# Half-position scans: lane sums completed by a product on TensorE and copied to their place by ScalarE

## What is computed

```python
# layer 0: four directions k over the positions (rows, columns, and both reversed)
dA = exp(dt[..., None] * A)
h = h * dA + (dt * u)[..., None] * B          # per position
y = einsum('bkdn,bkn->bkd', h, C)             # sum over the 16 states n
# the four y are brought back to row order and added; D * u is added for every direction
# layer 1: one direction over the positions
y = y + xin * D                               # then y * silu(z), out projection
```

## Time and profile before

| | us |
|---|---|
| median of 3 runs | 5808.86 (5805.29 to 5818.28) |
| profiled execution | 5813.53 |
| its span, first to last instruction | 5811.2 |
| TensorE busy (matmuls) | 4773.5 (82%) |
| VectorE busy | 4627.5 (80%) |
| GpSimd busy | 4111.9 (71%) |
| ScalarE busy | 3426.8 (59%) |
| granted TensorE clock, mean | 0.919 |

### The profile page before, as it was taken

One profiled execution on the slowest core, in us unless ns is written; L12 is line 12 of the kernel. 1 busy time (PEld: TensorE's weight loads), 2 busy tenths in 40 slices (PEclk: granted clock), 3 DMA queues, 4 the chain that ended last, 5 costly groups with the idle time before them and its releaser, 6 DMA issues. The chain is left out here.

```text
span 5811.2 us, 66280 instructions
## 1 busy us (share of the span) xinstructions
PE 4773.5 (82%) x20263; PEld 3262.6 (56%) x20263; DVE 4627.5 (80%) x4745; ACT 3426.8 (59%) x5199; POOL 4111.9 (71%) x3131
## 2 busy tenths in 40 slices
PE   5767686788889887778898887778988888777998
PEld 2222233236677745656676755665767764664787
DVE  5999947968999947986999965995999984996544
ACT  3434354337777756655777856764878765763222
POOL 3999926948999926975999953993999962993121
PEclk8898898888999998888999998888999999888999
DMA  5555505427778715645787833653878751662110
GB/s 213 213 210 190 182 28 185 155 93 268 264 267 280 248 46 191 216 152 187 265 270 263 281 116 128 222 188 124 282 265 275 259 195 55 212 219 86 41 49 28
DMA packets 340470, 1076.86 MB, mean 185 GB/s; under 512 B 31522, under 2 KB 123266, under 8 KB 332808
## 3 DMA queue, kind: packets, MB, share of 16 engines
q1 hardware_dynamic: 340104, 1072.52, 53.0%
HBM read 1058.72 MB, written 13.68 MB: 185 GB/s over the span
## 5 line engine op out<-in xcount | busy, mean ns | idle before, releaser
L958 PE MATMUL banks<-ident,prod 128*128 128x128 f32 x4752 | 780.9, 291 | 503.6 <-DVE prod L1172 388.5
L958 PEld LDWEIGHTS banks<-ident,prod 128*128 128x128 f32 x4752 | 566.0, 147 | 802.5 <-DVE prod L1172 616.6
L476 PE MATMUL banks<-prod,ident 128*128 128x512 f32 x972 | 563.7, 720 | 304.4 <-DVE prod L618 242.0
L1163 DVE TENSOR_TENSOR_SCAN banks<-banks,h 128x512 f32<-128x512 f32 x594 | 724.0, 1219 | 79.5 <-POOL h L1113 53.3
L1113 POOL TENSOR_TENSOR h<-lane,Bb 128x512 f32<-128x512 f32 x576 | 723.0, 1272 | 81.8 <-DMA Bb<-half_rows 57.3
L1054 ACT ACTIVATE banks<-lane,A 128x512 f32<-128x512 f32 x864 | 581.3, 686 | 283.5 <-DVE prod L1172 113.9
L534 ACT ACTIVATE banks<-delta_first,A 128x1024 f32<-128x1024 f32 x288 | 321.9, 1118 | 582.6 <-DVE prod L618 482.2
L1172 DVE TENSOR_TENSOR prod<-banks,half_C_a 128x512 f32<-128x512 f32 x792 | 548.0, 692 | 108.8 <-DVE banks L1163 2.9
L476 PEld LDWEIGHTS banks<-prod,ident 128*128 128x128 f32 x972 | 195.6, 219 | 665.4 <-DVE prod L618 414.0
L992 PE MATMUL banks<-Cb,w_a 128*128 128x256 f32 x2304 | 553.8, 380 | 0.0
L1123 POOL TENSOR_TENSOR h<-h,half_C_a 128x512 f32<-128x512 f32 x360 | 461.4, 1282 | 81.6 <-DVE h L1163 64.9
(11 more groups left out here) (382 smaller groups left out, 10936.2 us busy)
## 6 DMA issues: line engine op xcount, KB each, us to landing
Bb<-half_rows SPq DMA_DIRECT2D x576, 512.0 KB, 4.4
Cb<-half_rows SPq DMA_DIRECT2D x288, 512.0 KB, 4.5
w_a<-w_in SPq DMA_DIRECT2D x256, 576.0 KB, 6.3
half_C_a<-half_rows SPq DMA_DIRECT2D x160, 512.0 KB, 6.6
Bb<-rows SPq DMA_DIRECT2D x144, 512.0 KB, 4.2
Cb<-rows SPq DMA_DIRECT2D x144, 512.0 KB, 3.8
w_b<-w_in SPq DMA_DIRECT2D x128, 576.0 KB, 6.5
C_first<-rows SPq DMA_DIRECT2D x40, 1024.0 KB, 8.1
```

The lines of the kernel that those rows point to most:

```text
L476: mm = eng.matmul(ps[:, c, :], m.ident[:, :], src[:, cols(c)], start=n == 0, stop=added(s) == (i + 1) * N, skip_group_check=True)
L958: mm = eng.matmul(ps[:, 0, at], src[:, at], m.ident[:, :], start=n == 0 and k == 0, stop=added(s) == (i + 1) * N, is_transpose=True, skip_ ...
L1163: eng.tensor_tensor_scan(flip(to), flip(slot(s)), flip(m.dBu[:, s % DRIVES, :]), initial, ALU.mult, ALU.add).then_inc(st.scanned, 1)
```

## The change

`back` gets a fifth product: the transposed-back sum stays open in its PSUM group, and a full product with the identity, or with the identity scaled by D, adds the base (`u`, `xin` or the sum so far) to it. ScalarE makes the scaled identity (`scale`, a new resident tensor `scaled`, behind `copy_sum` in step 3) for the lanes that have a D term, 6 of 24 in layer 0 and all of layer 1. `take` moves from VectorE to ScalarE, behind the decay of step 8 (TAKE_AT was 7), and is a plain copy from the bank to its place. For the turned directions the order of positions in the bank stays as it is, and both the base on TensorE and the destination on ScalarE are read and written through a view with a stride of 32 elements. The waits for the previous user of the same place (`taken`, TILES lanes back) move to TensorE.

```diff
-    COPY_AT, BACK_AT, TAKE_AT, SUM_AT, DELTA_AT = 3, 4, 7, 8, 4
+    COPY_AT, BACK_AT, TAKE_AT, SUM_AT, DELTA_AT = 3, 4, 8, 8, 4
...
@@ back, on TensorE
                 for k in range(HALF // P):
                     at = slice(k * P, (k + 1) * P)
-                    mm = eng.matmul(bank("sum", i)[:, at], m.turned_sum[:, at], m.ident[:, :], start=k == 0,
-                                    stop=k == HALF // P - 1, is_transpose=True, skip_group_check=True)
-                mm.then_inc(st.back, 1)
+                    eng.matmul(bank("sum", i)[:, at], m.turned_sum[:, at], m.ident[:, :], start=k == 0, stop=False,
+                               is_transpose=True, skip_group_check=True)
+                x, j, c = lane(i)
+                if x.scale is not None:
+                    eng.wait_ge(st.scaled, scaled(i) + 1)
+                if i >= TILES:
+                    eng.wait_ge(st.taken, i - TILES + 1)
+                eng.matmul(x.view(bank("sum", i)), (m.ident if x.scale is None else m.scaled)[:, :], x.base(j, c), start=False,
+                           stop=True, skip_group_check=True).then_inc(st.back, 1)
...
@@ ScalarE
+            def scale(i):
+                x, j, _ = lane(i)
+                if x.scale is not None:
+                    if scaled(i):
+                        eng.wait_ge(st.back, i)
+                    eng.activation(m.scaled[:, :], m.ident[:, :], ACT.Identity, scale=x.scale(j)).then_inc(st.scaled, 1)
+
+            def take(i):
+                x, j, c = lane(i)
+                eng.wait_ge(st.back, i + 1)
+                eng.activation(x.to(j, c), x.view(bank("sum", i)), ACT.Copy).then_inc(st.taken, 1)
...
                     decay(s)
                     if i and n == COPY_AT:
                         copy_sum(i - 1)
+                        scale(i - 1)
+                    if i and n == TAKE_AT:
+                        take(i - 1)
...
                 if s == STEPS - 1:
                     copy_sum(LANES - 1)
+                    scale(LANES - 1)
+                    take(LANES - 1)
...
@@ VectorE
-            def take(i):
-                x, j, c = lane(i)
-                eng.wait_ge(st.back, i + 1)
-                if i >= TILES:
-                    eng.wait_ge(st.taken, i - TILES + 1)
-                x.take(eng, j, c, bank("sum", i)).then_inc(st.taken, 1)
...
-                    if n == TAKE_AT and i:
-                        take(i - 1)
...
-                if s == STEPS - 1:
-                    take(LANES - 1)
...
@@ layer 0's views (input_tile and sum_tile are u and ys at [:, j, cols(c)])
+            def turned_tile(j, c):
+                w = HALF // HH
+                return ys[:, j, :].rearrange("p (h w) -> p w h", w=WW)[:, c * w:(c + 1) * w, :]
...
+            def turned(y):
+                return y.rearrange("p (w h) -> p w h", h=HH)
...
-                    order = [(0, take_first), (2, take_more), (1, take_turned), (3, take_turned)]
+                    order = [(0, Named(base=input_tile, to=sum_tile, scale=skip_0, view=plain)),
+                             (2, Named(base=sum_tile, to=sum_tile, scale=None, view=plain)),
+                             (1, Named(base=turned_tile, to=turned_tile, scale=None, view=turned)),
+                             (3, Named(base=turned_tile, to=turned_tile, scale=None, view=turned))]
```

More of the change, by code:

```diff
@@ L732, in lane, with scaled @@
         return directions[d], i % TILES, c
+    def scaled(i):
+        return sum(lane(b)[0].scale is not None for b in range(i))
     held = [m.held[:, b, :] for b in range(HELD)]
@@ L2223, in build @@
                 ("kin", [P, CT, 3 * RANK], F32), ("kout", [P, C], F32), ("A0", [P, K0 * N * CT], F32),
-                ("A1", [P, N * DT1], F32), ("w0x", [P, K0, CT, BC + R0], F32), ("lowk", [P, K0 * C + DI], F32),
+                ("A1", [P, N * DT1], F32), ("w0x", [P, K0, CT, BC + R0], F32), ("lowk", [P, K0 * C + DI], F32), ("scaled", [P, P], F32),
                 ("proj1", [P, FT, RANK], F32), ("w1x", [P, DT1, BC + R1], F32)])
@@ L2237, in build @@
                        "back", "taken", "loaded", "hidden", "gelu", "down", "evicted", "accumulated", "ahead",
-                       "w1_0", "w1_1", "w2_0", "w2_1", "aside", "gates", "row", "late_row", *(f"b{i}" for i in range(4)), *(f"c{i}" for i in range(N // 2)))
+                       "w1_0", "w1_1", "w2_0", "w2_1", "aside", "gates", "row", "late_row", "scaled", *(f"b{i}" for i in range(4)), *(f"c{i}" for i in range(N // 2)))
         s_scan.b = [s_scan[f"b{i}"] for i in range(4)]
@@ L2316, in first_image, with plain @@
                     lane_scans(p, scan_tensors(scans, "first"), s_scan, directions, lanes, rows, turn=(u, ut))
+            def plain(y):
+                return y
             def half_scan_tensors(stack, name):
@@ L2404, in shared_scans, with tile, skip @@
                     w_out = tensors(nc, scans, [(f"w_out_{name}", [P, DT1, C], F32)])[f"w_out_{name}"]
-                    def take_tile(eng, t, c, y):
+                    def tile(t, c):
+                        return xin[:, t, cols(c)]
+                    def skip(t):
                         d = VEC["D1"][0] + t
-                        return eng.scalar_tensor_tensor(out=xin[:, t, cols(c)], in0=xin[:, t, cols(c)],
-                                                        scalar=m.vec[:, d:d + 1], in1=y, op0=ALU.mult, op1=ALU.add)
+                        return m.vec[:, d:d + 1]
                     def decay_1(t, n):
@@ L2415, in shared_scans @@
                     mamba = [Named(kts=[xin[:, t, :] for t in range(DT1)], wx=lambda t: m.w1x[:, t, :], rank=R1,
-                                   turned=False, reverse=False, A=decay_1, dt_at=K0 * C, take=take_tile)]
+                                   turned=False, reverse=False, A=decay_1, dt_at=K0 * C, base=tile, to=tile, scale=skip,
+                                   view=plain)]
                     guests = [(slice(0, QUARTER), slice(L - QUARTER, L))]
@@ L2425, in shared_scans, with input_tile, sum_tile, skip_0 @@
                         p.last = Named(all=s_out.all + s_moved.all)
[L2427 to L2434, removed]
-                w = HALF // HH
-                v = ys[:, j, :].rearrange("p (h w) -> p h w", w=WW)[:, :, c * w:(c + 1) * w]
-                return eng.tensor_tensor(v, v, y.rearrange("p (w h) -> p h w", h=HH), ALU.add)
+            def input_tile(j, c):
+                return u[:, j, cols(c)]
+            def sum_tile(j, c):
+                return ys[:, j, cols(c)]
+            def turned_tile(j, c):
+                w = HALF // HH
+                return ys[:, j, :].rearrange("p (h w) -> p w h", w=WW)[:, c * w:(c + 1) * w, :]
+            def skip_0(j):
+                return m.Dsum[:, j:j + 1]
+            def turned(y):
+                return y.rearrange("p (w h) -> p w h", h=HH)
             def decay_0(k):
@@ L2448, in scans @@
                     g = Named(g, un=un, x=m.x, **expert_tensors(fused, name + "0"))
-                    order = [(0, take_first), (2, take_more), (1, take_turned), (3, take_turned)]
+                    order = [(0, Named(base=input_tile, to=sum_tile, scale=skip_0, view=plain)),
+                             (2, Named(base=sum_tile, to=sum_tile, scale=None, view=plain)),
+                             (1, Named(base=turned_tile, to=turned_tile, scale=None, view=turned)),
+                             (3, Named(base=turned_tile, to=turned_tile, scale=None, view=turned))]
                     directions = [Named(kts=[(ut if k % 2 else u)[:, t, :] for t in range(CT)],
                                         wx=lambda t, k=k: m.w0x[:, k, t, :], rank=R0, turned=k % 2 == 1,
-                                        reverse=k >= 2, A=decay_0(k), dt_at=k * C, take=take) for k, take in order]
+                                        reverse=k >= 2, A=decay_0(k), dt_at=k * C, **take) for k, take in order]
                     guests = [(slice(q, q + QUARTER), slice(q, q + QUARTER)) for q in range(0, L - QUARTER, QUARTER)]
```

## The result

| | before | changed |
|---|---|---|
| median of 20 runs each, us | 5815.6 (5805.3 to 5824.4) | 5826.1 (5810.5 to 5836.1) |
| ratio, 95% interval | 1 | 1.0017 (1.0009 to 1.0025) |
| profiled execution, us | 5813.5 | 5824.5 |
| VectorE busy, us | 4627.5 | 4573.0 |
| ScalarE busy, us | 3426.8 | 3517.6 |

The account below looks back on a forecast made before the run. VectorE was taken to set the pace, with ScalarE's chain to scan 9 as long or nearly so in lanes without evictions. The terms summed to +19.6 us, giving 5828 against a median of 5808.9; range 5795 to 5870.

Parts of the forecast that it names:

- scan 9 in first halves of layer 1, no eviction: First-half lanes with nothing else between delta and scan 9: ScalarE already the bound, +0.53 us each in 24 lanes, +12.7.
- scan 9 in plain second halves, no eviction: Second-half lanes of layer 0: scan 9 at 6.05 us after the delta's end in place of 5.74, 21 lanes, +6.5.
- takes waiting for a late product inside a stretch: After a stretch at the lower clock, takes wait for late turned-back sums and products: some 3.3 us a stretch, +10.
- second-half plain lanes with an eviction: Second-half lanes where VectorE evicts before scan 9 gain the whole 0.58 us: 12 lanes, -7.0.
- turned take on ScalarE: ScalarE's copy writing SBUF with a stride of 32 elements: bounds 0.58 and 1.01 us, the upper taken, +11.
- scan 9 in turned second halves, no eviction: Second-half lanes of directions 1 and 3: the slow strided copy adds 0.43 us where ScalarE is the bound.
- strided product: TensorE's added product in turned lanes, moving operand strided: bounds 0.87 and 3.5 us, 0.87 taken.
- evictions of layer 1: Layer 1 lanes where VectorE evicts or accumulates before scan 9: 9 second-half lanes gain 0.63 us each, -5.7.
- last lanes of layer 0: Last lane of a layer 0 stretch, where TensorE runs without a pause and ScalarE waits for it: +0.87 each, +2.6.
- ends of stretches: Eviction and accumulation no longer follow VectorE's take: 1.5 us sooner, 1.1 with the slow copy, -7.7.
- the chain: ScalarE's queue from VectorE's delta to decay 9, for which scan 9 waits: the take adds 0.53 us to it.
- The case that I had set beside it: Strided product at 1.7 us: turns some 0.8 us later in five lanes a stretch, +12 to +17, inside the range.

Follow-up runs that it names:

- e4: The kernel before with one more ScalarE copy of 128x512 (result unused) behind decay 8 of every lane but a stretch's first: 1.0037 of the kernel before.
- e1: The changed kernel with ScalarE's take moved from behind decay 8 to behind decay 10: 0.9955 of the kernel before.
- e11: The changed kernel, take still behind decay 8, with the Gelu pair of step 8 one step later: 0.9938 of the kernel before.
- e6: The changed kernel with TensorE's base in turned lanes read without a stride, ScalarE's take still writing with it: 1.0001 of the kernel before.
- e3: The changed kernel with the take back on VectorE behind scan 7 as a plain copy, TensorE's product kept: 1.0048 of the kernel before.
- e2: The changed kernel with contiguous base and destination in turned lanes (the turning back left out): 0.9975 of the kernel before.
- e5: e1 with turned lanes as in the kernel before (no product, VectorE adds): 0.9957 of the kernel before.
- e7: e3 without strides in base and destination (the turning back left out): 1.0015 of the kernel before.
- e9: e5 with the Gelu pair of step 8 and its first down product one step later: 0.9939 of the kernel before.
- e10: The kernel before with the Gelu pair of step 8 one step later, nothing else: 0.9985 of the kernel before.

## Why the prediction was right

Forecast 5828 against 5808.9, +0.33%, with chances of 0.61 for slower and 0.29 for no difference; measured +0.17% (0.09 to 0.25), at the border of the two. The mechanism is the forecast's. That the time itself came out at 5826.1, so near 5828, is luck: the change costs 10.5 us and not 19.6, and the kernel before came out at 5815.6 in 20 runs, 6.7 above the three that the forecast was added to. Among the terms, too, errors of both signs met. Terms in us over the profiled executions; "scan 9" is its start counted from the delta's end:

| term | forecast | in the trace |
|---|---|---|
| scan 9 in first halves of layer 1, no eviction | +0.53 | +0.51 to +0.54 in all 12 |
| scan 9 in plain second halves, no eviction | at 6.05 | at 6.03 to 6.05 in 16 of 21, later in 5 |
| takes waiting for a late product inside a stretch | +10 | 21.1 us of waiting in 15 lanes, 15.1 of it in plain lanes |
| second-half plain lanes with an eviction | -0.58 each | -3.5 in 6 |
| idle time of scans behind decays | 110 | 101 |
| scan 9 released by a decay | in some 75 lanes | in 70 |
| turned take on ScalarE | 1.01 | 1.03 to 1.08 |
| scan 9 in turned second halves, no eviction | +0.74 | +0.78 to +0.82 |
| strided product | 0.87 | 1.70 |
| evictions of layer 1 | -0.63 in 9 lanes, -5.7 | -1.0 |
| last lanes of layer 0 | +2.6 | +4.5 |
| first lanes of the stretches, which have no take | 0 | +4.3 (-0.9 to +3.3) |
| ends of stretches | -7.7 | -10.8 |
| sum over the six stretches | +19.6 | +30.3 |

**Right: the chain.** The steps from the delta to scan 9 hold to 0.1 us, and e4, e1 and e11 show it from three sides: a copy added there, the take moved behind it, the Gelus moved behind decay 9. One small slip in the text of the forecast changes nothing: a take's place was used last three lanes ago in layer 0, six only in layer 1.

**Wrong: the strided product.** I kept both ends and took 0.87 us, "the row of the same engine". It was 1.70, the ratio of ScalarE's two rows (2.02/1.04, 1.94). The case that I had set beside it, +12 to +17 us by turns that come later still, was not what happened, though the trace's sum lies near it: takes in turned lanes waited 6.0 us inside the stretches, and 2.8 in e6, which has no stride on TensorE. The stride's 8.4 us by the lanes (e6) came in the last lanes and ends of layer 0 and in evictions of turned second-half lanes. There the forecast had a gain of 0.58 us, and four of six lanes lost 0.45 to 0.59. The evictions' longer wait for down products as a whole (16.0 us in place of 3.1) is mostly not the stride's: e6 has 12.9 us of it.

```profile
DVE prod L1211 <- PE banks L1003: 12.9, 7, 3.4
```

The page "SBUF — State Buffer" of the Trainium skill (section "Door 1: The DMA port swizzle") charges an access that enters a new line of 16 bytes. The trace agrees by now for three engines: ScalarE writing 1.07 against 0.58 us, TensorE's moving operand 1.70 against 0.87, VectorE writing 1.03 against 0.67 in e3.

**Wrong: the late products.** They were put at +10 us. The takes waited 21.1, and 15.1 of it in plain lanes, where no operand has a stride; in e6 and e2 the plain lanes of layer 0 have 13.4 and 13.9. So this term was too small for another reason than the stride. Which one, no run shows. With the take behind decay 10 (e1) no take inside a stretch waits.

**Wrong: the evictions of layer 1.** The accumulation that follows runs 1.83 us where it ran 1.18, in six of the nine lanes, and 1.52 where it ran 0.95 in the other three. VectorE reaches it 0.65 us sooner, and it then ends no sooner, or 0.08 us sooner in those three. Before, then after, with GpSimd's two products:

```profile
2330.61 3.20 POOL L1113 TENSOR_TENSOR h<-half_du_a,Cb 128x512 f32<-128x512 f32 x2
...
2331.51 1.18 DVE L1196 TENSOR_TENSOR late_x<-late_x,prod 128x768 f32<-128x768 f32 x1
```

```profile
2336.45 3.20 POOL L1141 TENSOR_TENSOR h<-half_du_a,Cb 128x512 f32<-128x512 f32 x2
...
2336.70 1.83 DVE L1217 TENSOR_TENSOR late_x<-late_x,prod 128x768 f32<-128x768 f32 x1
```

Measured from the start of GpSimd's pair VectorE's instruction ends at 2.08 us in both. So what was gained ahead of it is spent in it. The last section has what this shows of the two engines.

**Wrong, and in the other direction: the time.** The sum was +19.6, the trace's stretches say +30.3, and 20 runs say +10.5. Part of the difference is a gain that I did not forecast. At the end of a layer 0 stretch VectorE no longer holds take, eviction and accumulation in a line, so TensorE stands still for 1.37 us and not 4.42 before the next stage, and in the changed kernel its clock is then still at the upper level (2.4 GHz). The next stage's first twelve products, before, then after, and the granted clock (the last column but two) of the 8.4 us from there in each:

```profile
2063.65 8.43 PE L1559 MATMUL banks<-big,mean_mat 128*128 128x512 f32 x12 [4.42 <-PEq L802]
```

```profile
2069.31 5.39 PE L1576 MATMUL banks<-big,mean_mat 128*128 128x512 f32 x12 [1.37 <-PEq L807]
```

```profile
2063.60:2072.00 8.40, 8.35 (x13) 3.57 (x14) 1.88 (x3) 3.11 (x4) 2.80 (x3) 0.63 0.89 287
```

```profile
2069.20:2077.60 8.40, 8.29 (x20) 3.77 (x21) 3.77 (x6) 5.22 (x8) 3.89 (x3) 1.00 0.72 227
```

This is the first of three such hand-overs, and the one with the largest difference: the other two have 0.80 and 0.75 before, and 1.00 in the changed kernel. The shorter pause does not always keep the clock up: with the same 1.37 us four of the six hand-overs of e1 and e11 have 0.80.

The stages between a layer 0 and a layer 1 stretch lasted 160.2 us in the mean of the seven profiles in which VectorE holds the last take of layer 0 (before, e3, e4, e5, e7, e9, e10; 158.0 to 161.5), and 158.2 in the six in which ScalarE has it (154.2 to 160.4). That is 2 us three times. All time outside the stretches is 2474 to 2491 us in the seven, 2483.5 in the mean, and 2467 to 2481 in the six, 2474.3 in the mean. So about 9 us of the 18.8 may go with the change. By the scatter of the profiles that is uncertain by some 8 us (e4, e5 and e9, at 2474 to 2476, lie among the six), and no run was made for it. The rest is this pair of profiles: that of before, 2490, lies at the upper edge of its kind, that of the changed kernel, 2472, below the mean of its own. With 9 us the stretches' +30.3 would make +21, the runs say +5 to +15. Whether the stretches of the profile of before, taken once, were short by as much was not tried. How the 10.5 us of the times come out of the 30.3 of the stretches therefore stays open in part.

## What to carry to other kernels

Before work is moved from the bound engine to an idle one, look for the place in the receiver's queue and not at its load: ScalarE was busy 79% of a layer 0 stretch, and the same copies cost 0.6% more of the whole time ahead of a Gelu pair than behind it (1.0017 against 0.9955). The slack is read from the last event that both engines share (here the delta) to the next instruction that the bound engine waits for. And a view with a stride in SBUF had a price on each of the three engines that read or wrote through it here. Where VectorE read the stride in PSUM and wrote SBUF in runs of 16 elements, it paid nothing (0.66 us, as the plain add).

## What the runs showed of the hardware

- An element-wise stride of 128 bytes in SBUF makes an instruction 1.5 to 2 times as long: ScalarE's write 1.07 against 0.58 us, TensorE's moving operand 1.70 against 0.87, VectorE's write 1.03 against 0.67, for 128x512 in 4-byte elements.
- VectorE's accumulation into `late_x` (128x768, both inputs in SBUF) took 0.95 to 1.84 us depending on how long before the end of a GpSimd product it began, and GpSimd's next product then took 1.97 to 2.06 us for 1.27. The accumulation into `x` never took over 0.96 us, but none began more than 0.1 us before the end of a GpSimd product. The products that began in it, some 0.2 us behind its start, took 1.83 us, in 12 cases in each of the two profiles. These 12 and the 9 with `late_x` are all the half-position GpSimd products above 1.5 us. The page "SBUF — State Buffer" of the Trainium skill says in its section "🔬 SBUF: two separate sides" that a VectorE instruction with two SBUF inputs and a GpSimd instruction that reads SBUF take turns at one pair of ports for a whole instruction. The trace agrees in both cases.
- The granted clock over the 8.4 us behind the hand-over from layer 0's scans was 0.63 to 0.83 in the mean in all 21 cases with a pause of TensorE of 4.2 to 4.6 us (seven profiles). Behind a pause of 0.9 to 1.4 us (six profiles) it was 1.00 in 14 of 18 cases and 0.80 in the other four.
